# Form 0 of the left factor for layer 1: by a DMA load and a ScalarE copy from the third pair on, in place of a TensorE select

## What is computed

```python
for W in (W0, W1, W2):
    xk = relu(einsum('bmd,bhd,mhk->bkd', x0, xk, W))   # k = 64
    outs.append(sum(xk, axis=2))
```

## Time and profile before

| | |
|---|---|
| median of 3 runs | 337.7 us (336.69 to 337.79) |
| the profiled execution | 335.4 us, span 333.5 us |
| busy in the span | TensorE 301.6, VectorE 266.1, GpSimd 246.3, ScalarE 144.3 us |
| granted TensorE clock | 1.00 throughout |

### The profile page before, as it was taken

The page is one execution under the profiler, slowest core; times in us unless marked ns, Lnnn a source line. Parts: engine busy times, 40 slices in busy tenths (PEclk is TensorE's granted clock), DMA queues, the critical chain, the costliest instruction groups (busy, mean ns, idle before and its releaser), DMA issues.

```text
span 333.5 us, 4735 instructions
## 1 busy us (share of the span) xinstructions
PE 301.6 (90%) x1498; PEld 115.1 (35%) x1498; DVE 266.1 (80%) x117; ACT 144.3 (43%) x862; POOL 246.3 (74%) x162
## 2 busy tenths in 40 slices
PE   0078787998999999999999999999999999999996
PEld 0044332453234333323333333333333334333444
DVE  0025939998999999999999999999999988971301
ACT  1001210316617724593489248824971386213012
POOL 5777777786888977897879797978892996938000
DMA  6286978969744996289838963795177502300000
GB/s 188 34 266 118 335 187 243 362 121 332 307 77 106 260 353 120 73 274 390 169 87 255 365 100 85 245 374 123 48 199 280 135 25 67 94 2 0 0 0 2
DMA packets 55169, 56.72 MB, mean 170 GB/s; under 512 B 37894, under 2 KB 43912, under 8 KB 51944
## 3 DMA queue, kind: packets, MB, share of 16 engines
q1 hardware_dynamic: 42088, 40.87, 37.7%
q10 hardware_dynamic: 8960, 14.49, 16.3%
q0 software_dynamic: 4096, 1.06, 3.2%
HBM read 41.33 MB, written 2.10 MB: 130 GB/s over the span
## 4 chain that ended last, share of the span: by engine, by line
PE 76%; DVE 12%; DMA 5%; issue 3%; POOL 2%; ACT 1%; SPq 0%; ACTq 0%; DVEq 0%
PE result L659 67%; DVE z_vector L603 6%; DVE z_vector L610 5%; PE left L696 2%; POOL gathered_rows L334 2%; DMA r_forms<-x_rows 2%; PE y_psum L741 1%; DMA xj_forms<-x_sb 1%; PE result L711 1%; PE y_psum L711 1%; PE result L717 1%; PE y_psum L717 1%; DMA gathered_rows<-table,row_index 1%; DMA x_rows<-gathered_rows 1%; DMA table_base<-base 1%
## 5 line engine op out<-in xcount | busy, mean ns | idle before, releaser
L659 PE MATMUL result<-z_vector,w_sb 128*64 128x512 f32 (+2 forms) x1064 | 209.8, 542 | 9.8 <-DVE z_vector L610 5.7
L603 DVE TENSOR_TENSOR z_vector<-left,r_forms 128x4096 f32<-128x4096 f32 (+3 forms) x44 | 168.3, 3868 | 10.4 <-PE left L696 8.0
L334 POOL DMA_INDIRECT gathered_rows<-table,row_index x128 | 121.4, 949 | 37.5 <-issue 35.1
L350 POOL TENSOR_TENSOR z_pool<-r_forms,xj_forms 128x2048 f32<-128x2048 f32 (+2 forms) x29 | 124.2, 4308 | 20.2 <-DMA xj_forms<-x_sb 13.8
L659 PEld LDWEIGHTS result<-z_vector,w_sb 128*64 128x64 f32 x1064 | 75.4, 137 | 137.8 <-issue 110.9
L610 DVE TENSOR_TENSOR z_vector<-left,r_forms 128x2048 f32<-128x2048 f32 (+3 forms) x52 | 90.1, 1788 | 22.5 <-DMA r_forms<-x_rows 18.5
L423 ACT ACTIVATE x_sb<-x_sb 128x16 f32<-128x16 f32 x360 | 71.5, 200 | 6.4 <-issue 6.4
L423 ACT ACTIVATION_READ_ACCUMULATOR x_sb<-x_sb 128x1 f32 x360 | 67.3, 187 | 0.0
L659 PE MATMUL result<-z_pool,w_sb 128*64 128x512 f32 (+2 forms) x232 | 49.9, 570 | 0.0
L415 ACT ACTIVATE x_sb<-result 128x512 f32<-128x512 f32 (+2 forms) x27 | 14.8, 549 | 64.8 <-PE result L659 52.9
L396 ACT ACTIVATE left<-xj_forms 128x512 f32<-128x512 f32 (+2 forms) x36 | 18.6, 545 | 30.9 <-DMA xj_forms<-x_sb 12.8
(11 more groups left out here) (41 smaller groups left out, 46.2 us busy)
## 6 DMA issues: line engine op xcount, KB each, us to landing
r_forms<-x_rows SPq DMA_DIRECT2D x24, 1024.0 KB, 8.0
r_forms<-x_rows SPq DMA_DIRECT2D x8, 768.0 KB, 5.9
xj_forms<-x_sb ACTq DMA_DIRECT2D x24, 256.0 KB, 8.2
h_form<-x_rows SPq DMA_DIRECT2D x12, 256.0 KB, 3.9
xj_form<-x_sb ACTq DMA_DIRECT2D x12, 256.0 KB
gathered_rows<-table,row_index POOLq DMA_INDIRECT x128, 3.2
r_forms<-x_rows SPq DMA_DIRECT2D x4, 512.0 KB, 5.5
x_rows<-gathered_rows SPq DMA_DIRECT2D x24, 64.0 KB, 3.1
```

The lines of the kernel that those rows point to most:

```text
L334: nc.gpsimd.indirect_dma_start(gathered_rows[:, half % GATHERED, g], None, table, bass.IndirectOffsetOnAxis(ap=row_index[:, at:at + 1], ax ...
L350: nc.gpsimd.tensor_tensor(z_pool[:, unit % NZP, :, :, 0:columns(p)], r_forms(q, p)[:, :, s0:s1], xj1_forms[form_buffer(n, p)][:, :, 0:colu ...
L603: nc.vector.tensor_tensor(z_vector[:, unit % NV, :, 0:s1 - s0, 0:columns(p)], left[:, bank, :, 0:columns(p)].unsqueeze(2).broadcast_to([12 ...
L659: done = nc.tensor.matmul(result_of(n, p)[K * t:K * t + K, 0:columns(p)], weights, z[:, t, 0:columns(p)], start=first, stop=last)
```

## The change

`BY_LOAD` now holds, beside all of layer 2, layer 1 of every pair from `SELECTED` = 2 on. Those stages' form 0 comes by `load_xj0` and `copy_xj0`, all through the one buffer `xj0_form`; TensorE's select stays for pairs 0 and 1. In ScalarE's round with p + 1 >= 2, `load_xj0(1, p + 1)` is issued ahead of `load_xj1(1, p + 1)`, the sums over d of layer 2 are cut into two halves, and between them come `copy_xj0(1, p + 1)` and the issue of `load_xj0(2, p)`, which stood behind `relu(1, p)`.

```diff
-BY_LOAD = [(2, _p) for _p in range(NP - 2)] + [(1, NP - 1), (2, NP - 2), (2, NP - 1)]
+SELECTED = 2
+BY_LOAD = [_stage for _stage in LAYERS if _stage[0] == 2 or _stage[1] >= SELECTED]
...
-                        if n == 0:
+                        if n == 0 and p <= SELECTED:
                             act.wait_ge(selected, p)
                         for t in range(2):
-                            if n == 1:
-                                act.wait_ge(xj0_loaded[t], 16 * p)
+                            if (n + 1, p - 1) in BY_LOAD:
+                                act.wait_ge(xj0_loaded[t], 16 * (BY_LOAD.index((n + 1, p - 1)) + 1))
...
-            def sum_d(n, p, copied):
+            def sum_d(n, p, copied, part=0, parts=1):
 
                 act.wait_ge(x_ready[n], p + 1)
-                for b in range(SAMPLES[p]):
+                for b in range(SAMPLES[p] * part // parts, SAMPLES[p] * (part + 1) // parts):
...
             def load_xj0(n, p):
 
                 act.wait_ge(x_ready[n - 1], p + 1)
-                if n == 1:
-                    act.wait_ge(z_square_used, NP)
-                elif p > 0:
-                    act.wait_ge(left0_copied, 2 * BY_LOAD.index((2, p - 1)) + 2)
+                load = BY_LOAD.index((n, p))
+                if load > 0:
+                    act.wait_ge(left0_copied, 2 * load)
                 for t in range(2):
                     rows = x_sb[n - 1][K * t:K * t + H, 0:columns(p)]
-                    home, loaded = (xj0_form, xj0_loaded) if n == 2 else (xj0_last, xj0_last_loaded)
-                    act.dma_start(home[:, t, 0:columns(p)], rows.unsqueeze(1).broadcast_to([H, DELTAS, columns(p)])
-                                  ).then_inc(loaded[t], 16)
+                    act.dma_start(xj0_form[:, t, 0:columns(p)],
+                                  rows.unsqueeze(1).broadcast_to([H, DELTAS, columns(p)])
+                                  ).then_inc(xj0_loaded[t], 16)
 
             def copy_xj0(n, p):
                 before = LAYERS[LAYER_AT[n, p] - 1]
                 for t in range(2):
-                    if n == 2:
-                        act.wait_ge(xj0_loaded[t], 16 * (p + 1))
-                    else:
-                        act.wait_ge(xj0_last_loaded[t], 16)
+                    act.wait_ge(xj0_loaded[t], 16 * (BY_LOAD.index((n, p)) + 1))
...
                 relu(1, p)
-                load_xj0(2, p)
+                if p + 1 < SELECTED:
+                    load_xj0(2, p)
                 if p > 0:
                     copy_xj1(2, p - 1)
                 relu(0, p + 1)
-                if p + 1 == NP - 1:
+                if p + 1 >= SELECTED:
                     load_xj0(1, p + 1)
                 load_xj1(1, p + 1)
-                if p + 1 == NP - 1:
+
+                if p > 1:
+                    sum_d(2, p - 2, x_sb[2], 0, 2)
+                if p + 1 >= SELECTED:
                     copy_xj0(1, p + 1)
+                    load_xj0(2, p)
                 if p > 1:
-                    sum_d(2, p - 2, x_sb[2])
+                    sum_d(2, p - 2, x_sb[2], 1, 2)
```

More of the change, by code:

```diff
@@ L171, in build @@
         late2 = from_spare(N2 * LATE).rearrange("p (k c) -> p k c", k=N2)
-        xj0_last = z_square
         y_sb = h_form[0:1, 0].rearrange("o (t b) -> o t b", t=2)
@@ L193, in build @@
         xj0_loaded = [sem(f"xj0_loaded_t{t}") for t in range(2)]
-        xj0_last_loaded = [sem(f"xj0_last_loaded_t{t}") for t in range(2)]
         left0_copied = sem("left0_copied")
@@ L424, in sum_d @@
                                                 accum_out=d_sums[:, n, START[p] + b:START[p] + b + 1])
-                done.then_inc(x_summed[n], 1)
+                if part == parts - 1:
+                    done.then_inc(x_summed[n], 1)
             def load_xj1(n, p):
@@ L456, in copy_xj0 @@
                 for t in range(2):
-                    if n == 2:
-                        act.wait_ge(xj0_loaded[t], 16 * (p + 1))
-                    else:
-                        act.wait_ge(xj0_last_loaded[t], 16)
+                    act.wait_ge(xj0_loaded[t], 16 * (BY_LOAD.index((n, p)) + 1))
                     act.wait_ge(z_vector_ready, 2 * VECTOR_BEFORE[before] + 3 + t)
-                    home = xj0_form if n == 2 else xj0_last
-                    nc.scalar.activation(left[:, 0, t, 0:columns(p)], home[:, t, 0:columns(p)], ACT.Copy
+                    nc.scalar.activation(left[:, 0, t, 0:columns(p)], xj0_form[:, t, 0:columns(p)], ACT.Copy
                                          ).then_inc(left0_copied, 1)
```

## The result

The changed kernel took 347.2 us (median of 4 runs, 344.13 to 348.54), the kernel before 337.7 us (4 runs, 336.69 to 337.79). The ratio is 1.0285, its 95% interval 1.0221 to 1.0348: slower by some 9.5 us. The forecast was 339.8 us, with 343.8 as its upper end, so the sign was right and the size was not. In the experiments, the time of one kernel scatters by 1 to 8 us from one execution to the next, and the ratios leave out executions more than 1.5% above the fastest of their kernel.

The account below looks back on a forecast made before the run. VectorE was taken to bound the kernel to about 215 us, TensorE after. +3.0 - 0.46 - 0.25 + 0.6 + 0.3 - 1.06 = +2.1 us on the median 337.7 gave 339.8 us, range 336.4 to 343.8.

Parts of the forecast that it names:

- VectorE bounds the first part: Up to about 215 us VectorE sets the time, one pair per 33.2 us; from then to the end TensorE does.
- Pair 2's first unit: VectorE's start moves from 76.24 to 79.2, waiting for form 0's copies, timed as the other form's had been: +3.0 us.
- rival A: Nothing lost at pair 2 if the second load lands by 75.5: 334.5 to 336.2 us, faster; chance 0.12.
- Pair 3's h copy: Layer 2's form 0 load, issued later beside big loads, makes ScalarE's copy of h late: +0.6 us, bounds 0 and 1.2.
- the steady pairs: Pairs 4 to 7: form 0 ready 2.2 us early, ScalarE's next copy of h barely in time; +0.3 us taken.
- margin of 0.1 us: In steady pairs ScalarE's copy of h is done at 186.35, and VectorE wants it at 186.46.
- 1.21 us for two: ScalarE's time to issue two load DMAs in steady pairs; the added form 0 issues were costed at 1.21 us.
- It repeats in every second pair at most: A missed copy of h delays VectorE, but the next round starts from TensorE's time, so not every pair slips.
- rival C: ScalarE's loop becomes the bound once load landings reach 7 us: +5 to +9 us, 343 to 347; chance 0.10.
- the tail's select: The sixth removed select, at 237.08 in TensorE's gapless stretch, gives back its whole time: -1.06 us.
- Provided that VectorE stays ahead: Condition for the tail's select: VectorE's unit is made by 242.8, and TensorE wants it at 244.0.

Follow-up runs that it names:

- e5: The changed kernel once more, as control; 344.4 us, ratio 1.0271 to the kernel before.
- e9: Against the kernel before, only pair 2's select replaced by load and copy (beside pair 8, as before); 341.0 us, ratio 1.0165.
- e14: e9 without ScalarE's 32 sums over d of layer 0's pair 2; 340.9 us, ratio 1.0175 to the kernel before.
- e6: The changed kernel without layer 2's sums over d on ScalarE, one small copy instead; 343.8 us, ratio 1.0217 to the kernel before.
- e7: The changed kernel with layer 1's form 1 loads issued behind the first half of layer 2's sums; 342.2 us, ratio 1.0189 to the kernel before.
- e11: The changed kernel with pair 2's select kept and layer 1's form 1 loads issued behind the first half-sums; 338.3 us, ratio 1.0041 to the kernel before.
- e8: The changed kernel with relu 0 and its form 0 load ahead of relu 1 in ScalarE's round; 342.7 us, ratio 1.0190 to the kernel before.
- e12: The changed kernel with selects kept up to pair 6, only pair 7 (and 8) by load; 336.4 us, ratio 1.0021 to the kernel before.
- e13: e9 plus 12 spare matmuls on TensorE while it waits for pair 2's first product; 340.4 us, ratio 1.0128 to the kernel before.

## Why the prediction was wrong in size

**Right.** VectorE bounds the first part and the selects there cost little more than its waits of 0.46 and 0.63 for them, which went; two selects are left; the h copy at 96.08 has no idle time ahead of it. Pair 2's first unit: +3.0 forecast by the row of the same place, with the copies done 7.0 us after the relu's end; they were done 6.05 us after it, and idle is 3.76 where 1.66 had been, +2.1 (1.7 and 2.2 in e5 and e9). From issue to copy it was 3.5 and 4.8 us here, so rival A, which needed 2.7, was out of reach, as the rows of before had it. "DMA: Bandwidth & Descriptors" in the Trainium skill, section "Anatomy of one DMA", gives an estimate of 2.6 us for such a load, by its fit for GpSimd's path; no load of this size landed as fast in the rows shown.

**Wrong 1, "Pair 3's h copy", 0.6 forecast, 3.0 measured** (3.5 in e5, 3.9 in e9), outside my bounds of 0 and 1.2. I followed one load, that of layer 2's form 0, and asked when it lands. The stage that was late was another: form 1's two loads, issued behind the two new ones, reached their copies some 5 us later than before, counted from the relu, ScalarE stood in front of them in its fixed order, and 6 us of sums come after that. The prediction named the later form 1 for GpSimd only, and did not expect its landing to go from 4.4 to 9.3 us. e14 shows the end of the path: without those sums the wait is gone.

**Wrong 2, the steady pairs, 0.3 forecast, 3.5 measured** (2.3, the tail included, by e5 less e6). The margin of 0.1 us follows from its rows and should have been read as a warning; the term under it was mis-sized. "1.21 us for two", taken twice, gave 2.4 for four issues. Four in a row held ScalarE for 3.2 us in one round (the idle before the first sum) and 4.6 in another; e7, which only parts them, removes nearly all of the waits, and e11 does it in the time. "It repeats in every second pair at most" was wrong too: the wait for h came in three rounds in a row (1.90, 0.92, 1.90). The outcome lies just above rival C's 343 to 347; its mechanism, landings over 7 us, was not the cause for form 0, which landed in 3.5 to 4.3 us in the full rounds and was always there before its copy. Layer 2's form 1, which took 8.5 to 12.2 us, did hold relu 1, but e8 took relu 0 out from behind it and the waits for h stayed. What C had right is that ScalarE's own sequence becomes the bound.

**Wrong 3, the tail's select, -1.06 forecast, +2.3 measured** (0.7 in e5). "Provided that VectorE stays ahead": it did not (h 1.90; form 0 1.42, of which 0.96 stood there before), and GpSimd's product came 1.95 us after TensorE wanted it. By the order of issues, form 1's load for layer 2 starts later by what ScalarE lost; in e11 it is issued 2.6 us later from the mark than before, and GpSimd starts on it 2.9 us later. No run at the usual level took that load or GpSimd's share apart, so this link is read from the traces and not tested. e12, which removes only that select, shows 1.0021, no gain, by itself.

**By chance.** 2.7 us of the profiled span, at 40 to 50 us, ahead of everything that was changed; it is not in e5's.

No version tried beats the kernel before; e12 and e11 come nearest, e12 with an interval that reaches 0.9999.

## What to carry to other kernels

Before adding work to an engine that only serves others, list its whole order for one round and give each step its earliest time: a load added ahead of another delays that one's consumers too, on every engine, and what stands behind them in order. A margin of tenths of a microsecond, made of issues costed one by one, counts as spent. Taking matmuls away from an engine that waits elsewhere pays only if nothing else of its inputs moves.

## What was not expected of the hardware

- DMA issues by ScalarE: two took 1.21 us in most places (1.90 and 1.99 in two places of the kernel before). The third and fourth right behind them took 1.82, 1.88, 2.12, 2.25, 2.64 and 3.21 us together in six rounds of one execution of the changed kernel, and 1.48 in e7 with 2.2 us between. In the last round (at 275.03) they took 1.27 us, and 1.25 in the one such place of the kernel before (at 264.00). So four in a row are not enough by themselves. In five of the six slow rounds SyncE issued a DMA at the same time (as at 173.72, 209.66 and 242.70), in the sixth (108.34) it did not, and in the last round it issues none; what makes the difference is open. Parting the issues was enough to be rid of it.
- Two loads of 256 KB landed in 4.4 us, and in 9.3 us once two more of the same size were issued right ahead of them and the big loads followed sooner behind (8.3 to 8.8 in e5, e13 and e14); which of the two does it is open.
- TensorE after 4.41 us of idle: 32 matmul records took 9.67 us, 7.03 at full clock; the granted clock was 0.88 over 72 to 100. It cost no time that e13 could show, since another wait covered it. The same thing at 42.68, after 2.68 us of idle, was not covered: 16 records took 4.50 us and not 2.80, and this 1.7 us is in the 2.7 by which VectorE's next unit, which waited for the select behind them, came later.
